# Comparing, sorting and merging both groups of a pair in joint instructions, in a one-core perceiver layer

## The reference, cut to what matters

```python
def _focus(x, focusing_factor):
    x = jnp.abs(jnp.where(x >= 0, x, LEAKY_SLOPE * x)) + EPS
    nrm = x.mean(axis=-1, keepdims=True)
    return jax.nn.softmax(jnp.log(x) * focusing_factor, axis=-1) * nrm

def _topk_sparsify(x):          # x: rows of one head, 16 wide; KEEP = 11
    _, idx = jax.lax.top_k(jnp.abs(flat), KEEP)
    ...                         # all but the KEEP largest become 0

k = _focus(k @ Wk.T, focusing_factor)
kh = _topk_sparsify(_to_heads(k))
k_mean = kh.mean(axis=1)
kv = jnp.einsum('bnc,bnd->bcd', kh / sqrt_l, vh / sqrt_l)
```

## Time and profile before

| | us |
|---|---|
| median of 3 runs (lowest, highest) | 476.8 (476.25, 477.83) |
| the profiled execution | 476.32 |
| its span, first to last instruction | 474.6 |
| VectorE busy | 447.5 (94%) |
| TensorE products busy | 384.5 (81%) |
| ScalarE busy | 361.0 (76%) |
| mean granted TensorE clock | 0.942 of full speed |

### The profile page before, as it was taken

The page is one execution under the profiler, slowest core; times in us unless marked ns, Lnnn a source line. Parts: engine busy times, 40 slices in busy tenths (PEclk is TensorE's granted clock), DMA queues, the critical chain, the costliest instruction groups (busy, mean ns, idle before and its releaser), DMA issues.

```text
span 474.6 us, 5931 instructions
## 1 busy us (share of the span) xinstructions
PE 384.5 (81%) x1877; PEld 304.1 (64%) x1880; DVE 447.5 (94%) x684; ACT 361.0 (76%) x950; POOL 7.3 (2%) x22
## 2 busy tenths in 40 slices
PE   1997659998898998997997997991999899628664
PEld 1876547786786876886886885891976455214333
DVE  6799999999999999999999999999998889899994
ACT  2569985997997987997978978885438668666764
POOL 2001000000000000000000000000000000000000
PEclk9998778999999999999999999997899999867978
DMA  7990000230230230140140041032020000000001
GB/s 234 355 298 0 1 0 1 78 100 1 81 98 1 63 115 1 45 134 0 42 130 8 18 130 32 1 94 85 0 90 0 0 3 0 1 0 0 23 23 44
DMA packets 27070, 27.65 MB, mean 58 GB/s; under 512 B 1184, under 2 KB 26784, under 8 KB 27040
## 3 DMA queue, kind: packets, MB, share of 16 engines
q1 hardware_dynamic: 26736, 27.27, 17.9%
q0 software_dynamic: 160, 0.01, 0.0%
q10 hardware_dynamic: 144, 0.00, 0.0%
HBM read 26.22 MB, written 1.05 MB: 57 GB/s over the span
## 4 chain that ended last, share of the span: by engine, by line
DVE 79%; PE 10%; ACT 6%; issue 3%; DMA 1%; SPq 0%; ACTq 0%; DVEq 0%
DVE focus_words L1289 8%; DVE mask L1369 8%; DVE focus_words L1269 8%; DVE sorted L1325 4%; DVE level L1295 4%; DVE level L1296 4%; DVE sorted L1326 4%; DVE merge L1338 4%; PE bank L815 3%; DVE sorted L1198 3%; DVE sorted L1331 2%; DVE sorted L1330 2%; DVE keymax L1328 2%; DVE merge L1336 2%; DVE amax L1167 2%
## 5 line engine op out<-in xcount | busy, mean ns | idle before, releaser
L815 PE MATMUL bank<-WkT,rows_T 128*128 128x256 f32 x512 | 128.6, 399 | 30.5 <-ACT rows_T L433 30.5
L815 PEld LDWEIGHTS bank<-WkT,rows_T 128*128 128x128 f32 x512 | 97.8, 199 | 48.4 <-ACT rows_T L433 35.9
L910 PE MATMUL bank<-ctx_words,focus_words 128*128 128x257 f32 x512 | 115.0, 382 | 3.5 <-ACT focus_words L532 3.5
L910 PEld LDWEIGHTS bank<-ctx_words,focus_words 128*128 128x128 f32 x512 | 99.3, 197 | 16.0 <-ACT focus_words L532 5.5
L520 ACT ACTIVATE focus_words<-focus_words,shift,ff 128x256 f32<-128x256 f32 x136 | 79.8, 590 | 0.6
L486 ACT ACTIVATE focus_words<-bank 128x256 f32<-128x256 f32 x136 | 50.1, 381 | 28.0 <-PE bank L815 28.0
L532 ACT ACTIVATE focus_words<-focus_words,row_scale 128x256 f32<-128x256 f32 x136 | 56.2, 514 | 11.5 <-DVE row_scale L1282 11.5
L433 ACT ACTIVATE rows_T<-bank 128x512 f32<-128x512 f32 x78 | 44.2, 595 | 18.2 <-PE bank L788 18.2
L788 PE MATMUL bank<-ident,ctx_words 128*128 128x128 f32 x256 | 38.4, 279 | 3.5 <-DMA ctx_words<-in_ctx_dram 2.8
L1369 DVE TENSOR_TENSOR mask<-focus_words,fifth 128x2048 bf16<-128x2048 f32 x17 | 39.0, 2292 | 0.5
L788 PEld LDWEIGHTS bank<-ident,ctx_words 128*128 128x128 f32 x256 | 31.6, 144 | 11.5 <-DMA ctx_words<-in_ctx_dram 5.2
(11 more groups left out here) (198 smaller groups left out, 577.3 us busy)
## 6 DMA issues: line engine op xcount, KB each, us to landing
ctx_words<-in_ctx_dram SPq DMA_DIRECT2D x32, 512.0 KB, 3.9
ctx_words<-in_L_ffn_gate_w_dram SPq DMA_DIRECT2D x2, 1024.0 KB, 8.0
ctx_words<-in_L_ffn_up_w_dram SPq DMA_DIRECT2D x2, 1024.0 KB, 9.0
xs<-in_x_dram SPq DMA_DIRECT2D x4, 256.0 KB, 5.0
ctx_words<-in_L_ffn_down_w_dram SPq DMA_DIRECT2D x2, 512.0 KB, 10.0
ctx_words<-in_L_ffn_down_w_dram SPq DMA_DIRECT2D x1, 1024.0 KB, 4.6
out_dram<-xs SPq DMA_DIRECT2D x3, 256.0 KB, 2.1
gateT<-in_L_attn_W_qkv_dram SPq DMA_DIRECT2D x1, 512.0 KB, 6.4
```

What stands on the lines that cost most here:

```text
L815: ins = pe.matmul(proj_bank[m][:, t * D:(t + 1) * D], rows_T[:, m % 2, 2 * t + k, :], WT[:, k, :], start=(k == 0), stop=(k == KT - 1))
L910: ins = pe.matmul(sum_bank[k][:, 0:GW], heads_half(expo[slot][:, t, :], k), ctx_ring[:, s, t, :], start=(s == 0 and t == 0), stop=(s == PE ...
```

## The change

In all pairs but the first and the last, VectorE compares, sorts and merges both groups in one set of instructions over sixteen tiles (`sort_fours_of_both`), with the maxima first. For that the keys of both groups lie side by side (planes 1 and 2; the exponentials of the odd slot move to plane 4), and the keys of d are made at the end of the pair before. `level1` and `sorted4` get room for sixteen tiles; `rank` and `low8` lie in `level1`'s place, with three rank rows less. Row maxima, their logarithms and the shifts are made for both groups at once. ScalarE's order in these pairs is new: logarithms of c at the end of the pair before, all four quads of c copied ahead of the exponentials of a, those of b later, the lifts of d and the weight quads ahead of `scale_rows(a)`; the lifts of d also in the first pair. TensorE's and the transfers' programs are as before. Some places of the tail's tiles move along (`q_step`, `q_bf16`, `gate_fp4`, `zr`, two planes swapped). The core of the diff:

```diff
         lifted = [plane[0], plane[3]]
-        key = [plane[4], plane[1]]
-        expo = [plane[2], plane[5]]
+        key = [plane[2], plane[1]]
+        expo = [plane[4], plane[5]]
+        keys_of_both = focus_words[:, T * D:3 * T * D].rearrange("p (t r c) -> p t r c", t=2 * T, r=4)
...
-        level1 = sb("level1", [P, T, 4, 64])
-        sorted4 = sb("sorted4", [P, T, 5, 64])
+        level1 = sb("level1", [P, 2 * T, 4, 64])
+        sorted4 = sb("sorted4", [P, 2 * T, 5, 64])
-        low8 = sb("low8", [P, 2 * T, 4, HEADS])
-        rank = sb("rank", [P, 2 * T, 13, HEADS])
+        level1_words = level1[:, :, :, :].rearrange("p t r c -> p (t r c)")
+        rank = level1_words[:, 0:20 * T * HEADS].rearrange("p (t s c) -> p t s c", t=2 * T, s=10)
+        low8 = level1_words[:, 20 * T * HEADS:28 * T * HEADS].rearrange("p (t s c) -> p t s c", t=2 * T, s=4)
...
+        rowmax = sb("rowmax", [P, 2 * T])
+        keymax = sb("keymax", [P, 2 * T])
+        lnmax = sb("lnmax", [P, 2 * T])
+        shift = sb("shift", [P, 2 * T])
...
             return 1 if n == 0 else 1 + (n + 1) // 2 if n < CGROUPS - 1 else n - CGROUPS // 2 + 2
 
+        def of_pair(n):
+
+            return slice(0, T) if n % 2 or n == 0 else slice(T, 2 * T)
+
+        def searched_alone(n):
+
+            return n <= 2 or n >= CGROUPS - 1
...
             def exponentials(n, s, tiles):
 
                 slot = (s + 1) % 2
+                first = of_pair(n).start
                 if tiles[0] == 0:
 
-                    act.wait_ge(rowmax_ready, n + 1)
-                    act.activation(lnmax[:, :], rowmax[:, slot, :], ACT.Ln, bias=EPS).then_inc(lnmax_done, 1)
-                    act.wait_ge(lnmax_done, n + 1)
-                    act.activation(shift[:, :], lnmax[:, :], ACT.Identity, scale=ff_neg[:, 0:1]).then_inc(shift_done, 1)
+                    if searched_alone(n) or n % 2:
+                        of, count = (of_pair(n), 1) if searched_alone(n) else (slice(0, 2 * T), 2)
+                        act.wait_ge(rowmax_ready, n + count)
+                        act.activation(lnmax[:, of], rowmax[:, of], ACT.Ln, bias=EPS).then_inc(lnmax_done, count)
+                        act.wait_ge(lnmax_done, n + count)
+                        act.activation(shift[:, of], lnmax[:, of], ACT.Identity, scale=ff_neg[:, 0:1])\
+                            .then_inc(shift_done, count)
                     act.wait_ge(shift_done, n + 1)
                     act.wait_ge(logs_done, n + 1)
...
                 b, c, d = a + 1, a + 2, a + 3
                 at = lambda n: (n - 1) % PER_BATCH
-                logarithms(a, at(a))
+                if a == 1:
+                    logarithms(a, at(a))
...
@@ -576,13 +592,36 @@
                     rows_to_sbuf(d, 2)
                     lift(d, 1, at(d))
                     rows_to_sbuf(d, 3)
-                    scale_rows(a, at(a))
+                    lift(d, 2, at(d))
+                    lift(d, 3, at(d))
+                else:
+                    rows_to_sbuf(c, 0)
+                    rows_to_sbuf(c, 1)
+                    logarithms(b, at(b))
+                    rows_to_sbuf(c, 2)
+                    rows_to_sbuf(c, 3)
+                    exponentials(a, at(a), ALL_TILES)
+                    lift(c, 0, at(c))
+                    rows_to_sbuf(d, 0)
+                    lift(c, 1, at(c))
+                    rows_to_sbuf(d, 1)
+                    if at(a) == 0:
+                        save_sums((a - 1) // PER_BATCH)
+                    lift(c, 2, at(c))
+                    lift(c, 3, at(c))
+                    rows_to_sbuf(d, 2)
+                    exponentials(b, at(b), FORE_TILES)
+                    rows_to_sbuf(d, 3)
+                    exponentials(b, at(b), HIND_TILES)
+                    for m in range(PAIRS):
+                        lift(d, m, at(d))
+                if not last:
                     if d in ATT_BEHIND:
                         q = ATT_QUADS + 2 * ATT_BEHIND.index(d)
                         weight_quad(q)
                         weight_quad(q + 1)
-                    lift(d, 2, at(d))
-                    lift(d, 3, at(d))
+                    scale_rows(a, at(a))
+                    logarithms(c, at(c))
                 scale_rows(b, at(b))
...
+                at = of_pair(n)
+                step(tt(level1[:, at, 0:4:2, :], k4[:, :, 0:4:2, :], k4[:, :, 1:4:2, :], ALU.min))
+                step(tt(level1[:, at, 1:4:2, :], k4[:, :, 0:4:2, :], k4[:, :, 1:4:2, :], ALU.max))
...
+            def join_fours(at):
+
+                settle(but=1)
+                step(tt(high[:, at], sorted4[:, at, 0:2, 0:32], sorted4[:, at, 0:2, 32:64], ALU.max))
+                settle(but=1)
+                step(tt(low[:, at], sorted4[:, at, 0:4, 0:32], sorted4[:, at, 0:4, 32:64], ALU.min))
+
+            def inner_twos(at):
+
+                step(tt(sorted4[:, at, 1, :], sorted4[:, at, 4, :], sorted4[:, at, 2, :], ALU.min))
+                step(tt(sorted4[:, at, 2, :], sorted4[:, at, 4, :], sorted4[:, at, 2, :], ALU.max))
+
+            def row_maxima(at, groups):
+
+                dve.tensor_scalar(rowmax[:, at].bitcast(I32), keymax[:, at].bitcast(I32), -HD, key_flip[:, 0:1],
+                                  ALU.bitwise_and, ALU.bitwise_xor).then_inc(rowmax_ready, groups)
+
...
+            def sort_fours_of_both(a):
+
+                both = slice(0, 2 * T)
+                settle()
+                dve.wait_ge(keyed, a + 2)
+                step(tt(level1[:, :, 1:4:2, :], keys_of_both[:, :, 0:4:2, :], keys_of_both[:, :, 1:4:2, :], ALU.max))
+                settle()
+                then(tt(sorted4[:, :, 3, :], level1[:, :, 1, :], level1[:, :, 3, :], ALU.max))
+                step(dve.tensor_reduce(keymax[:, :], sorted4[:, :, 3, :], AX.X, ALU.max))
+                step(tt(level1[:, :, 0:4:2, :], keys_of_both[:, :, 0:4:2, :], keys_of_both[:, :, 1:4:2, :], ALU.min))
+                settle(but=1)
+                row_maxima(both, 2)
+                settle()
+                step(tt(sorted4[:, :, 2, :], level1[:, :, 0, :], level1[:, :, 2, :], ALU.max))
                 step(tt(sorted4[:, :, 0:5:4, :], level1[:, :, 0:2, :], level1[:, :, 2:4, :], ALU.min))
+                settle()
+                inner_twos(both)
+                join_fours(both)
...
-                then(tt(rank[:, at, 10:12, :], rank[:, at, p2:p3 + 1, :], rank[:, at, t3:t1 + 1, :], ALU.max))
-                then(tt(row(12), row(10), row(11), ALU.min))
-                step(tt(fifth[:, at, :], row(12), row(p4), ALU.min))
+                then(tt(rank[:, at, p2:p3 + 1, :], rank[:, at, p2:p3 + 1, :], rank[:, at, t3:t1 + 1, :], ALU.max))
+                then(tt(row(p2), row(p2), row(p3), ALU.min))
+                step(tt(fifth[:, at, :], row(p2), row(p4), ALU.min))
...
             def pair(a, last):
 
-                b, c = a + 1, a + 2
+                b, c, d = a + 1, a + 2, a + 3
                 at = lambda n: (n - 1) % PER_BATCH
-                compare_pairs(a)
-                sort_fours(a)
-                make_keys(b, at(b))
                 if last:
+                    compare_pairs(a)
+                    sort_fours(a)
                     find_fifths(of_pair(a))
+                    settle()
                     compare_pairs(b)
-                else:
+                elif a == 1:
+                    compare_pairs(a)
+                    sort_fours(a)
+                    make_keys(b, at(b))
                     compare_pairs(b)
                     sort_fours(b)
+                    find_fifths(slice(0, 2 * T))
+                else:
+                    sort_fours_of_both(a)
                     find_fifths(slice(0, 2 * T))
                 make_mask(a)
                 if last:
@@ -1441,6 +1514,7 @@
                     make_keys(c, at(c))
                     settle()
                     apply_mask(b, at(b))
+                    make_keys(d, at(d))
```

More of the change, by code:

```diff
@@ L520, in exponentials @@
                     ins = act.activation(expo[slot][:, t, :], lifted[slot][:, t, :], ACT.Exp,
-                                         bias=shift[:, t:t + 1], scale=ff[:, 0:1],
+                                         bias=shift[:, first + t:first + t + 1], scale=ff[:, 0:1],
                                          accum_out=exp_sum[:, slot, t:t + 1])
@@ L552, in pair @@
                     tail_rows_to_sbuf("sums1", (proj_in_psum, PAIRS * (CGROUPS + 1)))
-                else:
-                    rows_to_sbuf(c, 0)
-                    rows_to_sbuf(c, 1)
-                exponentials(a, at(a), ALL_TILES)
-                logarithms(b, at(b))
-                if at(a) == 0:
-                    save_sums((a - 1) // PER_BATCH)
-                if last:
+                    exponentials(a, at(a), ALL_TILES)
+                    logarithms(b, at(b))
+                    if at(a) == 0:
+                        save_sums((a - 1) // PER_BATCH)
                     tail_rows_to_sbuf("sums2", (kv_in_psum, 1))
```

(26 more changed lines are left out.)

35 lines of the change are left out of this document (7 added, 28 removed).

## The result

| | before | after | after, second set |
|---|---|---|---|
| median, us | 476.7 | 537.5 | 537.7 |
| lowest, highest, us | 476.25, 477.83 | 533.18, 543.36 | 531.92, 541.16 |
| ratio to before, 95% interval | 1 | 1.124 [1.117, 1.132] | 1.122 [1.116, 1.127] |

The changed kernel is 61 us slower. The ratios leave out one execution of each set, which took over 1.5% longer than the fastest of its set.

What follows compares the result with a forecast made beforehand. The prediction took a loop through VectorE, ScalarE and TensorE to bound the changed kernel: 476.3 us before + 40.7 for the loop + 15.0 and 6.0 for TensorE's clock = 538 us, own range 528 to 547, 8 in 10 within 515 to 549.

Steps and rivals of the forecast that it cites:

- Who sets the pace: A loop through VectorE, ScalarE and TensorE, 41.5 us a pair, bounds the kernel instead of VectorE's own 36.3 us.
- VectorE's part: Compare and sort on VectorE, 11 instructions instead of 20: 0.5 us saved a pair, its own loop 36.3 us.
- The loop at full clock: Key sum of a to reciprocal 35.4 us, to next key sum 6.1; six intervals add 40.7 us.
- The clock, first gap: TensorE idles 6.5 us ahead of a's key sum and restarts at lower clock: 2.5 us a pair, 15.0 in all.
- The clock, second gap: TensorE idles 2.9 us ahead of d's first projection; clock falls in half the pairs, 2.0 us each, 6.0 in all.
- The sum: Profiled execution before, plus full-clock loop and both clock gaps: 476.3 + 40.7 + 15.0 + 6.0 = 538 us.
- The rival in which the clock holds: The loop closes as forecast, but TensorE's clock doesn't fall in its gaps: 517 us, chance 10%.
- What would show it: Reciprocals near 45 us apart, VectorE idle 5 to 9 ahead; ScalarE waits 8 or more ahead of c's third copy.

## Why the prediction was right, point by point

- *Who sets the pace.* That a loop takes the chain from VectorE was right: the unread products and ScalarE's order move the time, the joint instructions don't. That it goes through all three engines was not: the chain holds ScalarE, TensorE and a transfer. The prediction's own sum shows how near it was, since the row scales are ready 2.5 us behind the reciprocal and the lifts of d are through at 2.7. The reciprocal marks the rounds; it isn't a step of them.
- *VectorE's part.* First comparison to first merge of the fifths: 16.13 us (184.41 to 200.54), predicted 16.2. VectorE's own round: 36.30, predicted 36.3. Saved: 0.48 us a pair, predicted 0.5. The Trainium skill, VectorE: DVE Perf Modes, section on the TRN2 errata, gives a fixed part per instruction by which nine fewer would have saved an estimated 1.4 us; the durations in the trace agree with its formula (2.29 us for 2048 elements), the saving of 0.48 us doesn't, since an instruction starts before the duration of the one before is over (2.21 us behind it).
- *The loop at full clock.* From the key sum to the first exponential of a: 22.67 us, less the 1.40 us by which the key sum was longer than 7.22, is 21.3; predicted 21.1. From the reciprocal to the key sum: 6.31 us (126.20 to 132.51), and 7.41 with the weight quads (218.42 to 225.83); predicted 6.1 and 7.3. With both gaps filled the six intervals between reciprocals were 49.07, 42.42, 43.09, 43.48, 41.79 and 42.41 us, 262.3 in sum; predicted 49.65 and five of 41.5 with 4.2 of extras, 261.35. Less the 220.7 us of before that is 41.6 us, predicted 40.7: the first round was 0.6 us shorter than the sum of its steps, each of the others 0.2 to 0.4 longer. By medians the full-clock part is 519.1 - 476.7 = 42.4 us.
- *The clock, first gap.* The mechanism was right: idle 4.12 us in the first pair and 5.85 to 6.76 us from the second on, every time, and a slow key sum behind it (at 0.50 where the clock was read). The size was somewhat too large. The prediction took 2.5 us a pair, 15.0 in all, from two restarts in the trace of before; the six key sums of the loop took 1.4 to 3.1 us more than 7.22, 13.5 in sum, and the rounds of the profiled executions differ by as much. By medians it is 10.8. The Trainium skill, TensorE: Matmul & The Clock Gate, section on oscillation in real kernels, has the same mechanism for loops that wait for transfers; the trace agrees, with waits for another engine's instructions in the place of the transfers.
- *The clock, second gap.* Here the step was wrong in its count. The prediction let the clock fall in half of the pairs at 2.0 us. It fell in five of six, each time behind 3.10 us of idling, and cost 7.7 us by medians (7.5 by rounds) and not 6.0.
- *The sum.* By medians 476.7 + 42.4 + 10.8 + 7.7 = 537.6, against 476.3 + 40.7 + 15.0 + 6.0 = 538.0. The measured terms are differences between kernels, so they add up by construction. That the total is closer than its terms is luck: by medians 1.7 and 1.7 were missing and 4.2 was too much, by rounds 0.9 and 1.5 were missing and 1.5 was too much. The rival in which the clock holds, 517 us, is the kernel with both gaps filled, 519.1.
- *What would show it.* Rounds of 44.6 to 47.9 us behind the first (45 was named), and 8.2 to 11.5 us idle ahead of the reciprocal (5 to 9 was named, too little). The wait ahead of c's third copy is 6.67 us and not 8 or more: the logarithms of b, 1.91 us, stand in it. That was in the diff, and the prediction overlooked it; it costs nothing, since they fill waiting time.
- *What the prediction left out.* That the loop has two rungs, the early copies and the late exponentials of b. Either alone is dear: 538.4 us for the copies in the old order, 511.0 for the exponentials of b with the copies put back. The second figure holds falls of the clock, too. A kernel of the old order with only b's exponentials moved back wasn't tried, and neither was one with only the lifts of d ahead of `scale_rows(a)` in all pairs.

## What to carry to other kernels

Before an instruction is moved up in one engine's queue, follow what it waits for through the other queues, once round, until the chain comes back to the same instruction a round later; the longest such round, and not the busiest engine, sets the time. An engine that waits long isn't for that reason a part of the loop: VectorE waited 8 to 11 us in each round, and no step of the loop was its own. Here two copies of half a microsecond, put ahead of eight exponentials, were worth 62 us, and nine instructions saved on the busiest engine 0.5 us a pair. Where a loop does wait, look at what the waiting does to TensorE's clock: work without use in the gap can be cheaper than the gap.

## What the runs showed of the hardware that was not expected

- An idle time of 3.10 us, the same to 0.01 us, was followed by full clock in one pair and by the lower level in five, in the kernel with only the gap ahead of the key sum filled (full clock in the first of the six) and in both profiles of the changed kernel (full clock in the last). The profile of one pair doesn't tell how often it happens; all pairs together do.
- The changed kernel's executions scatter over 11 us, those of the kernel before over 3. In its first set an execution of 533.18 us had a mean granted clock of 0.904 and one of 538.46 us a clock of 0.882. With both gaps filled the scatter is 0.4 us.
- Added products made the kernel faster: 18.5 us in six rounds, for about twelve products ahead of a key sum and eight ahead of a projection.
